# Mixture stage: weights split into two float32r parts during an earlier stage, three products in place of one

## What is computed

```python
# layer 0: feed-forward, DFF 1376
gate = x @ W_gate + lora(...)
up = x @ W_up + lora(...)
hidden = silu(gate) * up
out = hidden @ W_down + lora(...)
# layer 1: mixture, 8 experts, width 512
expert_idx = argmax(x @ router_w, -1)
score = sigmoid(max(x @ router_w, -1))
xs = x * score
for e in range(8):
    xe = where(expert_idx == e, xs, 0)
    h = silu(xe @ gate_w[e]) * (xe @ up_w[e])
    out += where(expert_idx == e, h @ down_w[e], 0)
shared = silu(x @ shared_gate_w) * (x @ shared_up_w) @ shared_down_w
```

## Time and profile before

| what | us |
|---|---|
| runs | 3370.05, 3384.73, 3385.86; median 3384.73 |
| the profiled execution's own time | 3374.49 |
| its span, first to last instruction | 3372.7 |
| feed-forward, of the span | about 1075 to 1717 |
| mixture, of the span | about 2895 to 3365 |

### The profile page before, as it was taken

One profiled execution on the slowest core, in us unless ns is written; L12 is line 12 of the kernel. 1 busy time (PEld: TensorE's weight loads), 2 busy tenths in 40 slices (PEclk: granted clock), 3 DMA queues, 4 the chain that ended last, 5 costly groups with the idle time before them and its releaser, 6 DMA issues. The chain is left out here.

```text
span 3372.7 us, 47754 instructions
## 1 busy us (share of the span) xinstructions
PE 2988.1 (89%) x16274; PEld 2015.9 (60%) x16274; DVE 1621.0 (48%) x3128; ACT 1270.7 (38%) x3276; POOL 627.1 (19%) x701
## 2 busy tenths in 40 slices
PE   6999958888883899999979987899999999899998
PEld 4676623333231777777745554788888888544443
DVE  5556556766770321111136665566667666311222
ACT  2434406655562211111125553455565555211111
POOL 1000031223222000000010011333333333110332
PEclk9999979988995999999989998999999999899999
DMA  1000057775653200000010011011121110522342
GB/s 63 25 25 19 13 142 136 143 153 128 147 118 103 84 14 13 14 13 14 7 47 25 25 57 56 32 45 50 60 79 51 51 50 26 191 63 88 105 177 75
DMA packets 129471, 229.71 MB, mean 68 GB/s; under 512 B 17061, under 2 KB 34789, under 8 KB 129296
## 3 DMA queue, kind: packets, MB, share of 16 engines
q1 hardware_dynamic: 98352, 174.73, 18.9%
q0 software_dynamic: 13936, 31.98, 3.2%
q10 hardware_dynamic: 17008, 20.67, 1.9%
HBM read 167.68 MB, written 61.00 MB: 68 GB/s over the span
## 5 line engine op out<-in xcount | busy, mean ns | idle before, releaser
L1407 DVE TENSOR_REDUCE x_minus_max<-banks 128x2 f32<-128x1024 f32 x256 | 308.1, 1222 | 157.6 <-PE banks L1473 155.7
L1355 ACT ACTIVATE x_probs<-banks 128x512 f32<-128x512 f32 x512 | 272.4, 597 | 148.5 <-PE banks L1491 134.5
L580 ACT ACTIVATE a_probs<-banks,a_minus_max 128x128 f32<-128x128 f32 (+1 forms) x512 | 208.4, 430 | 97.0 <-DVE a_minus_max L665 96.4
L1491 PEld LDWEIGHTS banks<-x_stacked_q,x_stacked_k 53*128 53x128 f32 x512 | 64.0, 200 | 208.6 <-issue 156.5
L1491 PE MATMUL banks<-x_stacked_q,x_stacked_k 53*128 53x512 f32 x512 | 160.3, 526 | 28.5 <-ACT x_probs L1355 24.4
L2236 POOL TENSOR_TENSOR x_probs<-x_probs,x_inverse 128x512 f32<-128x512 f32 x128 | 133.1, 1040 | 266.5 <-DVE x_inverse L2442 266.5
L2300 ACT ACTIVATE x_probs<-banks,x_minus_max,x_rroot 128x256 f32<-128x256 f32 x256 | 142.9, 566 | 87.5 <-DVE x_minus_max L2408 87.5
L665 DVE TENSOR_REDUCE a_minus_max<-banks 128x2 f32<-128x512 f32 (+1 forms) x192 | 131.5, 685 | 84.2 <-PE banks L821 71.3
L1473 PE MATMUL banks<-x_stacked_k,x_stacked_q 51*128 51x512 f32 x512 | 135.3, 479 | 40.8 <-DVE x_whole L1424 12.9
L3071 PE MATMUL banks<-m_w,m_xT 128*128 x368 | 167.3, 598 | 3.2 <-issue 3.2
L1823 DVE TENSOR_TENSOR f_hT<-banks,f_silu 128x256 f32<-128x256 f32 (+1 forms) x88 | 37.2, 424 | 268.6 <-ACT f_silu L1736 268.6
(11 more groups left out here) (384 smaller groups left out, 7780.7 us busy)
## 6 DMA issues: line engine op xcount, KB each, us to landing
x_parts_dram<-x_parts SPq DMA_DIRECT2D x16, 1024.0 KB, 6.0
x_x<-x_after SPq DMA_DIRECT2D x24, 512.0 KB, 4.2
x_stacked_k<-x_parts_dram SPq DMA_DIRECT2D x96, 128.0 KB
x_stacked_q<-x_parts_dram SPq DMA_DIRECT2D x96, 128.0 KB
x_after<-a_z SPq DMA_DIRECT2D x16, 512.0 KB, 2.7
x_z<-x_after SPq DMA_DIRECT2D x16, 512.0 KB, 6.6
x_heads_dram<-x_heads_out SPq DMA_DIRECT2D x32, 256.0 KB, 4.7
x_after<-x_z SPq DMA_DIRECT2D x16, 512.0 KB, 3.4
```

Source lines behind the costliest of these rows:

```text
L580: ins = act.activation(probs[:, n % 3, i * width:(i + 1) * width], psum[uses.bank(use)][:, i * width:(i + 1) * width], ACT.Exp, bias=minus ...
L1355: act.activation(probs[:, n % 8, :], psum[at.bank(f"exp{n}")], ACT.Exp, scale=SCALE)\
L1407: dve.tensor_reduce(minus_max[:, c % 2, h % 4:h % 4 + 2, t], at.pair(use), AX.X, ALU.max, negate=True)\
L1491: ins = pe.matmul(psum[at.bank(use)], stacked[1][u][rows, h // 2, s * P:(s + 1) * P].bitcast(F32R), stacked[0][u][rows, h // 2, :].bitcast ...
```

## The change

The mixture's weights become float32r pairs, and its products three matmuls each. The pairs are made during the feed-forward: 30 pieces of 128 x 2048 (27 matrices and three of zeros), laid out on the host from the weights as they are, are loaded into the space of `raw_up_first` (two slots), rounded by ScalarE into `expert_high`, split by VectorE in place, and both parts stored to DRAM by GpSimd. Five pieces go in each sequence of turns 1 to 3, behind the hidden tiles 1, 3, 5, 7 and 9. In the mixture x and hT are split as well, for the shared tiles too; each weight load is 2 MB; gate, up and down of an expert are loaded and waited for apart, each as its own buffer part comes free. The three buffers with both parts take the room of `xT_all` in: it lies where expert 1's up and down parts will be, so these two are loaded when all 16 shared tiles are split. VectorE's order in a tile changes: the rest of hT comes between the statistics of y and its normalisation. Three semaphores of earlier stages (`weights_loaded`, `low_loaded`, `down_loaded`) live longer.

```diff
@@ feed_forward_lora
+        expert_rest = [raw_up_first[:, :, :].rearrange("p c n -> p (c n)")[:, k * KC * D:(k + 1) * KC * D] for k in range(2)]
+        expert_high = sb("expert_high", [P, KC * D])
+        EXPERT_PIECES_AT = ({1: 0, 3: 1, 5: 2, 7: 3, 9: 4}, {1: 5, 3: 6, 5: 7, 7: 8, 9: 9})
+        PER_TURN = 10
...
@@ gpsimd
-            with pool.Fori(0, TURNS) as turn:
+            def load_expert_piece(piece, slot):
+                pool.dma_start(expert_rest[slot], expert_raw[piece].rearrange("a p n -> (a p) n"))\
+                    .then_inc(expert_loaded[slot], 16)
+            def store_expert_piece(turn, c):
+                g = expert_piece(turn, c)
+                pool.wait_ge(expert_split, g + 1)
...
+                pool.dma_start(expert_parts[bass.ds(g, 1), 0].rearrange("a p n -> (a p) n"), expert_high[:, :])\
+                    .then_inc(expert_high_stored, 16)
+                pool.dma_start(expert_parts[bass.ds(g, 1), 1].rearrange("a p n -> (a p) n"), expert_rest[c % 2])\
+                    .then_inc(expert_rest_stored, 16)
+            def follow_expert_piece(turn, c):
+                g = expert_piece(turn, c)
+                pool.wait_ge(expert_high_stored, g * 16 + 16)
+                pool.wait_ge(expert_rest_stored, g * 16 + 16)
+                pool.sem_inc(expert_high_free, 1)
+                load_expert_piece(bass.ds(g + 2, 1), c % 2)
+            for k in range(2):
+                load_expert_piece(slice(k, k + 1), k)
+            pool.sem_inc(expert_high_free, 1)
...
+            with pool.Fori(1, TURNS) as turn:
                 for u in range(2):
+                    for j, c in EXPERT_PIECES_AT[u].items():
+                        store_expert_piece(turn, c)
+                        follow_expert_piece(turn, c)
                     norm_pool(core, norm, turn, u)
@@ scalar
+            def round_expert_piece(turn, u, j):
...
+                act.wait_ge(expert_high_free, g + 1)
+                high_part_act(act, expert_high[:, :], expert_rest[c % 2]).then_inc(expert_rounded, 1)
...
                     act.activation(silu[0:m, j % 3, :], psum[uses.bank(use)][0:m, 0:T], ACT.Silu).then_inc(silu_ready, 1)
+                    round_expert_piece(turn, u, j)
@@ vector
+            def split_expert_piece(turn, u, j):
...
+                dve.wait_ge(expert_rounded, expert_piece(turn, c) + 1)
+                subtract(dve, expert_rest[c % 2], expert_rest[c % 2], expert_high[:, :]).then_inc(expert_split, 1)
...
                         .then_inc(free[uses.bank(use)], 1)
+                    split_expert_piece(turn, u, j)
@@ mixture
-        w = sb("w", [P, BUFFERS, 3, KC, D])
+        w = sb("w", [P, BUFFERS, 3, 2, KC, D])
...
-                for m, key in enumerate(("g", "u", "d")):
-                    sp.dma_start(w[:, e % BUFFERS, m], weights[key][e].rearrange("(c p) n -> p c n", p=P))\
-                        .then_inc(expert_loaded[e % BUFFERS], 16)
+                for m, used in enumerate((gate_full, up_full, y_full)):
+                    if e == BORROWED and m == 1:
+                        sp.wait_ge(x_split, NT)
+                    if e == SHARED:
+                        sp.wait_ge(used, NT)
+                    if e >= BUFFERS:
+                        sp.wait_ge(used, done[e - BUFFERS])
+                    load_weight(e, m, expert_loaded[m][e % BUFFERS])
...
+            def round_x(t):
...
+                high_part_act(act, x_high[:, t % 2], source).then_inc(x_rounded, 1)
...
-                act.copy(hT[:, u], psum[XT + u].rearrange("p (c t) -> p c t", c=KC)).then_inc(hT_ready, 1)
+                high_part_act(act, hT_high[:, u], psum[XT + u].rearrange("p (c t) -> p c t", c=KC)).then_inc(hT_rounded, 1)
...
+            def rest_of_h(t):
...
+                subtract(dve, hT_rest[:, u], psum[XT + u].rearrange("p (c t) -> p c t", c=KC), hT_high[:, u]).then_inc(hT_ready, 1)
...
+                if 1 <= t < LAST:
+                    rest_of_x(t + 1)
...
                 if t >= 1:
                     give_y(t - 1)
+                rest_of_h(t)
+                if t >= 1:
+                    normalise(t - 1)
...
-                    ins = pe.matmul(psum[bank], parts[:, c, :], weight(buffer, m, c), start=c == 0, stop=c == KC - 1)
+                    ins = split_matmul(pe, psum[bank], [part[:, c, :] for part in parts],
+                                       [weight(buffer, m, part, c) for part in range(2)], start=c == 0, stop=c == KC - 1)
...
-                    for k in range(BUFFERS):
-                        pe.wait_ge(expert_loaded[k], needs[k])
...
+                pe.wait_ge(x_split, t + 1)
+                wait_expert(0, needs)
```

More of the change, by code:

```diff
@@ L1565, in ffn0_layout, with feed_forward_lora @@
     }
[L1568 removed]
+def feed_forward_lora(core, name, x_src, x_dst, weights, expert_raw, expert_parts):
     nc = core.nc
@@ L2675, in mixture_pads, with mixture_weights, mixture @@
     return pads
-def mixture(core, name, x_src, x_dst, base, slot_meta, weights):
+def mixture_weights(inputs):
+    import numpy as np
+    pieces = np.zeros((EXPERT_PIECES + 2, P, KC * D), np.float32)
+    for m, key in enumerate(("gate_w", "up_w", "down_w")):
+        for e in range(E + 1):
+            w = inputs["L1_ffn_" + key][e] if e < E else inputs["L1_ffn_shared_" + key]
+            pieces[e * 3 + m] = np.asarray(w).reshape(KC, P, D).transpose(1, 0, 2).reshape(P, KC * D)
+    return pieces
+def mixture(core, name, x_src, x_dst, base, slot_meta, parts_src, weights):
     nc, psum = core.nc, core.psum
@@ L2742, in mixture @@
         shared_loaded = ring_of("shared_loaded", 3)
-        expert_loaded = ring_of("expert_loaded", BUFFERS)
+        expert_loaded = [ring_of(f"expert_{part}_loaded", BUFFERS) for part in ("gate", "up", "down")]
         filled = sem("filled")
@@ L3051, in _, with weight @@
                     first_logits(t - 2)
-            def weight(slot, m, c):
+            def weight(slot, m, part, c):
                 if slot is None:
-                    return w[:, SHARED, m, c, :]
-                return w[:, bass.ds(slot, 1), m, c, :].rearrange("p a n -> p (a n)")
+                    return w[:, SHARED, m, part, c, :]
+                return w[:, bass.ds(slot, 1), m, part, c, :].rearrange("p a n -> p (a n)")
             def fact(k, s):
@@ L3082, in down @@
                     pe.wait_ge(y_ready, t - 1)
-                product(DOWN + u, hT[:, u], buffer, 2, y_full)
+                wait_expert(2, needs)
+                product(DOWN + u, (hT_high[:, u], hT_rest[:, u]), buffer, 2, y_full)
             chosen_flat = chosen_bf[:, :, :].rearrange("p t e -> p (t e)")
@@ L3121, in _ @@
                     pe.wait_ge(h_ready, t - 1)
+                wait_expert(1, needs)
                 product(UP + u, source, buffer, 1, up_full)
@@ L3126, in _ @@
                 if t >= 1:
-                    down(t - 1, previous)
+                    down(t - 1, previous, before_needs)
                 if t >= 1:
                     transpose_h(t)
-                previous, (buffer, needs) = buffer, following
-            down(LAST, previous)
+                previous, before_needs, (buffer, needs) = buffer, needs, following
+            down(LAST, previous, before_needs)
 def decoder_layers(nc, a, x, result):
@@ L3154, in decoder_layers @@
         feed_forward_lora(core, "f0", between[1], between[2],
-                          group("f0", "first", "gate", "up", "down", "B_gate", "B_up", "A_down", "B_down", "bias"))
+                          group("f0", "first", "gate", "up", "down", "B_gate", "B_up", "A_down", "B_down", "bias"),
+                          a["m1_all"], expert_parts)
         with ExitStack() as both:
@@ L3162, in decoder_layers @@
             cross_attention_grouped(core, "x1", between[3], a["ctxT"], between[4], half_way, x1_weights, early)
-        mixture(core, "m1", between[4], result, base, slot_meta, group("m1", "r", "g", "u", "d", "sg", "su", "sd", "table", "pads"))
+        mixture(core, "m1", between[4], result, base, slot_meta, expert_parts, group("m1", "r", "table", "pads"))
 def layout(inputs):
```

120 lines of the change are left out of this document (88 added, 32 removed).

## The result

The changed kernel takes 3484.3 us (median of 4 runs, 3482.0 to 3494.3) against 3380.9 us in the same comparison: ratio 1.031, 95% interval 1.029 to 1.034, slower as forecast, 16 us under the 3500. Its profiled execution has a span of 3480.4 us, 107.7 more.

| span in us | before | after |
|---|---|---|
| ahead of the feed-forward | 1075.1 | 1087.4 |
| feed-forward, to its last store | 638.4 | 783.2 |
| from there to the mixture | 1181.9 | 1185.2 |
| mixture | 477.3 | 424.6 |

The account below looks back on a forecast made before the run. TensorE, busy 89% of the span, was taken as the bound. Feed-forward loss 186 us less mixture gain 71 us made 115 us, 3489 us profiled and 3500 us as median of runs; range 3435 to 3600 us.

Parts of the forecast that it names:

- The serial chain: Feed-forward: five pieces per sequence run serially through one high buffer; TensorE starts 29.3 us late, 186 us lost in six.
- the tail: Feed-forward, after four cycles: one rounding, one subtraction and the last hidden tile's own 0.42, together 4.7 us.
- The quick-store rival: Feed-forward: the two stores run at the best rate seen, 160 us lost instead of 186, 3474 us; chance 0.13.
- C: Feed-forward: one piece's cycle of rounding, subtraction, two stores and hand-overs, 1.94 + 2.29 + 9.3 + 0.4 = 13.9 us.
- The clock: Feed-forward: after idling TensorE runs at 0.72 of full clock for 6 us, costing 1.7 us more per sequence.
- Products and shared tiles: Mixture: a product takes 2.80 us instead of 3.43, three per tile 8.40; 39 tiles give 74.1 us.
- Slot facts at nothing: Mixture: four register loads between up and down products could cost 0 to 3.6 us a slot; taken as 0.
- The little-gain rival: Mixture: register loads cost 3 us a slot, 69 of the 71 us won, 3569 us; chance 0.12.
- Loads of twice the size: Mixture: loads double to 6.3 MB per expert yet hide; the two load waits go, 3.2 us won.
- Base rows: Mixture: the wait for the first gather comes round again, 3.9 us lost, 7 more if weights stand ahead.
- First shared weight: Mixture: the first shared weight is 1 MB longer and lies ahead of four row loads, about 2 us lost.
- The pieces keep up: Feed-forward: the chain is hidden if C is under 6.6 us, leaving only the gain, 3314 us; chance 0.05.

Follow-up runs that it names:

- the spread kernel: The changed kernel with the same thirty pieces, five per sequence, split at places some 15 us apart: 3327.2 us, ratio 0.984 to the kernel before the change.

## Why the prediction was right, point by point

The sign, the mechanism and the size hold, but the sum was helped by luck, in errors that cancel: 186 - 71 = 115 forecast, 144.8 - 52.7 + 15.6 = 107.7 in the traces, and 12.3 of these are the scatter ahead of the feed-forward. Without them 95.4 are left.

- **The serial chain**: right, in each link (rounding 1.90 and subtraction 2.29, drawn on from the earlier trace rows as 1.94 and 2.29), and shown by moving it. The mis-sized term is the stores with their hand-overs, 9.3 + 0.4 us: they took 7.5 (11.7 less the other two). I had taken the queue's rate as its bytes over the share of its packets, 296 GB/s; a further megabyte took 2.55 us, 411 GB/s. Four cycles and the tail are 51.7 us (1380.38 to 1432.1) where I had 60.3. The quick-store rival was nearer, with C = 12.8. By the rule that the Trainium skill gives (DMA: Bandwidth & Descriptors, Anatomy of one DMA) C would be an estimated 11.4. The 11.8 measured agrees better with that than with any row I used.
- **The clock**: too small, and its other side was left out. TensorE starts 20.7 us late (51.7 against 31.0) and the sequence is 24.1 longer (144.8 / 6), so 3.4 are left where I had 1.7. In the sequence shown the part from line 1988 to the last down product takes 5.0 us more (1432.1 to 1462.4, where it was 1376.4 to 1401.7), with the clock at 0.50, its lower level, at first, where the earlier trace rows have 0.72 in the mean. But that slow stretch of the earlier trace rows, at the start of a sequence, is gone here: the clock is at 1.00 there (below), and the end of the SiLU of tile 1 follows the last store of rows after 14.1 us instead of 15.6.

```profile
1366.30:1372.00 5.70, 3.88 (x33) 3.88 (x34) 4.81 (x21) 0.13 (x1) 0.00 (x0) 1.00 0.24 93
```

- **Products and shared tiles**: right, 2.79 a product and 8.83 a tile (of the chain, 8.39 and 0.44). VectorE's hT came 0.6 us ahead of the x transposes, as forecast (0.5).
- **Slot facts at nothing**: wrong in size. Some 0.6 us a slot shows, and two loads moved bring the 9.27 forecast back (9.26). The little-gain rival had the mechanism, at a fifth of its price. By the Trainium skill's figure (DMA: Bandwidth & Descriptors, Latency and other measured facts), an estimated 2.4 us for four, they would have been hidden in 3.7; either they take longer or the cover is shorter, which no run separates.
- **Loads of twice the size**: right, no wait for an expert is left. **Base rows**: right, two tiles took 24.3 us (3240.83 to 3265.11) instead of 19.8: 4.5, forecast 3.9. **First shared weight**: nothing lost (28.2 us from the first row load to the first gate product, 28.4 before), forecast 2.
- **Not foreseen**: the hold under the scatters. The additions of y at 3100.38 and 3134.09 are 33.7 us apart where three tiles are 26.5: 7.2 us. Tiles and slots won 60 us, the load waits 3.2; less 4.5 and 7.2 that leaves 51.5, against 52.7.
- **"The pieces keep up"** has become true without a shorter chain: not C under 6.6 us, but some 15 us of room for each C.

## What to carry to other kernels

Work for idle engines is free only if its whole cycle, transfers and buffer release included, fits between two places where it is put; count that cycle before the busy time, and spread the pieces over the stage rather than over its idle stretch. When one link of such a chain is shortened, look at once for the wait that takes its place (here the load, then the queue). For a queue's rate use two transfers of different size in the trace, not its bytes over its share of time.

## What the runs showed of the hardware that was not expected

- Beside GpSimd's sixteen scatters of small rows (20 us) an addition that waits for TensorE came 3 to 6 us late in the kernels with split products, with the DMA engines 7% busy in one of them and 66% in another (the spread kernel); the hold moved with the scatters.
- Of three 1 MB transfers (a load and two stores) issued together into GpSimd's queue the last landed 9.9 us after its issue (median of thirty pieces); of two stores the second landed 6.1 after. In a stretch of two stores of the changed kernel the queue alone moved 391 GB/s (below).

```profile
1386.00:1390.00 4.00, 4.00 (x33) 3.89 (x32) 0.00 (x0) 0.00 (x0) 0.37 (x1) 1.00 0.96 391
```

- From the last store of the feed-forward to the mixture, in code that the change leaves alone, pass 1193 to 1195 us in the three kernels with spread pieces and 1182 to 1190 in the seven others. In the spread kernel 10.4 of its 13.3 more than in the kernel before lie right at the start, ahead of the next stage's first load (see the first experiment).
